# A state-space layer with routed experts: another order of its first tiles, gathers with a lead of four, and one store in five moved

## The chip, the core and the metric

The kernel runs on one core of one Trainium2 chip. Five engines work beside each other: TensorE (PE; PEld is its weight load), VectorE (DVE), ScalarE (ACT), GpSimd (POOL) and SyncE (SP, which here only issues DMAs). The metric is the device time of one execution in microseconds, lower is better. Before the change it is 276.38 us, the median of three runs (275.71 to 276.61).

## What is computed

Four sequences of 512 tokens, 128 wide. `u` is normalized, and two things are computed of it: a state-space layer (its core in the reference below) and a mixture of 16 experts of which each token takes two, with the weights of a softmax over its two best router scores; both are added to `u`.

```python
proj = u @ W_in   # split: z, x, Bg, Cg, dd_dt, dd_A, trap, angles
theta = jnp.cumsum(angles[:, :, None, :] * dt[..., None], axis=1)
K = _rope(Bn[:, :, None, :] + B_bias, theta)
Q = _rope(Cn[:, :, None, :] + C_bias, theta)
S1 = jnp.einsum('bcihn,bcjhn->bcijh', Qc, Kc) * g1c[:, :, None, :, :] * decay
y_inter = jnp.einsum('bcihn,bcih,bchpn->bcihp', Qc, jnp.exp(ell), Hprevs)
y = y + D[None, None, :, None] * x
y = y * jax.nn.silu(z)
return y.reshape(b, L, D_INNER) @ W_out
...
# of each expert e: layernorm((silu(xn @ W1[e]) * (xn @ W3[e])) @ W2[e]) * gamma[e] + beta[e]
```

## The kernel before

The 2048 tokens are 16 tiles of 128 for the state-space part. The expert part sorts the 4096 (token, expert) pairs into 40 blocks of 128 tokens: 32 of one expert, and 8 mixed ones (block 2, 7, 12, ...) of two experts with 64 tokens each. Everything is in one program for each engine, with the order written out by hand; engines wait for each other by semaphores (`wait_ge`), and each engine runs its own list in order.

Three stages follow each other. Up to about 24 us: normalization, router scores, projections. Then the routing on DVE (`one_hots`, `pick_experts`), which sorts the tokens: PE inverts the sort with `invert(k)` over two sets of one-hots, DVE makes of it the lists `gidx` (which token a block gathers) and `sidx` (where its result goes), and `blk_e` (which expert a block has), which starts SP's loads of weights (`load`, four sets in the buffers). Beside it ACT makes the decays of all 16 tiles: tiles 0 to 7 from PE's sums, 8 to 15 from rows that POOL masks (`cut_rows`); PE sums the angles (`sum_turns`), which DVE reduces to `theta` (`cut_turns`).

The third stage weaves tiles and blocks (`weave`, `iteration`): turn t computes tile t of the state-space part and two (even t) or three (odd t) blocks, `b0, b1, b2`. For a block: POOL gathers its tokens from DRAM (`gather`), PE turns it (`turn_block`), ACT copies it (`out_block`), PE multiplies by both up weights (`rise`: the first product goes to ACT's `silu`, the second to DVE's `product`), PE multiplies down (`down`), DVE normalizes (`norm_y`), POOL takes the root (`finish`), DVE scales (`shift_block`) and POOL stores (`store`). For a tile: PE projects (`project_x`, `project_bc`), ACT squares and makes sine and cosine (`squares`, `sines`), POOL `rms_pow` and `rot_sine`, DVE `norm_kq`, `rot_cosine` and `rotate`, PE turns keys and queries (`turn_kq`), then in the next turn `scores`, `inter`, `intra`, where `inter` needs POOL's `weigh_q`. `square_own` (POOL) and `diagonal` (DVE) complete a tile's decay.

Before the change, turn 0 is: block 0 up, tile 0's keys and queries turned, block 1 up, block 0 down. POOL gathers block b + 6 in block b's place (L664), in six buffers (`SLOTS`). The last stage adds the stored results to `acc` and writes the output.

## Time and profile before

| | us |
|---|---|
| median of three runs | 276.38 |
| profiled execution, its own time | 277.72 |
| its span, first to last instruction | 276.0 |
| PE busy | 245.0 (89%) |
| DVE busy | 222.7 (81%) |
| ACT busy | 146.2 (53%) |
| POOL busy | 205.7 (75%) |

The span is the profiled execution's; 1.7 us of its time lie outside it. PE's granted clock is full but for two stretches, 50 to 60 us (0.66 in the mean) and behind 250 us. Shares of the whole span say little of the stretches: the rows below are read by stretch and engine.

### The profile page before, as it was taken

The numbers are of one execution on the slowest core, as the hardware profiler recorded it, in microseconds if no ns is written. First come the engines' busy times: TensorE is split into PE (matmuls) and PEld (weight loads), VectorE is DVE, ScalarE is ACT, GpSimd is POOL, SyncE is SP. The second block draws the span as 40 slices with busy tenths as digits, with TensorE's granted clock in tenths as the row PEclk, the third lists the DMA queues.
The fourth block names the chain that finished last, engine by engine and source line by source line (L and its number), as shares of the span: only waits on it lengthen the run. The fifth ranks groups of instructions, "written<-read, shape, count | busy, mean of one in ns | idle before, by whom it ended". The sixth has DMA issues, their size and how long they took to land.

```text
span 276.0 us, 7214 instructions
## 1 busy us (share of the span) xinstructions
PE 245.0 (89%) x2091; PEld 216.0 (78%) x2094; DVE 222.7 (81%) x596; ACT 146.2 (53%) x492; POOL 205.7 (75%) x279
## 2 busy tenths in 40 slices
PE   2999997499999999999999999999999999998500
PEld 0857964498998898899989979997998899887300
DVE  4768998967979989896989879699889787976446
ACT  1765989546464463737354654636362746452033
POOL 8658997846898979788897978898688786656300
PEclk9999999779999999999999999999999999999855
DMA  6630836976869979878898988788889688870195
GB/s 160 208 114 8 269 119 197 290 200 171 239 224 236 297 219 299 285 226 237 242 285 238 288 255 241 252 239 257 276 238 300 198 269 243 250 200 21 33 296 145
DMA packets 68278, 60.48 MB, mean 219 GB/s; under 512 B 6544, under 2 KB 52240, under 8 KB 68240
## 3 DMA queue, kind: packets, MB, share of 16 engines
q1 hardware_dynamic: 65680, 54.78, 67.1%
q0 software_dynamic: 2560, 5.25, 6.5%
q8 instruction: 17, 0.28, 0.4%
q14 instruction: 21, 0.17, 0.2%
HBM read 55.22 MB, written 4.78 MB: 217 GB/s over the span
## 4 chain that ended last, share of the span: by engine, by line
PE 74%; DMA 6%; ACT 6%; POOL 6%; issue 3%; DVE 2%; SPq 1%; ACTq 0%; POOLq 0%; DVEq 0%
PE bank L897 19%; PE bank L942 10%; PE bank L892 5%; PE bank L838 5%; PE bank L830 4%; ACT decay L1063 3%; PE bank L865 3%; PE bank L813 3%; DMA decay<-l_dram 3%; PE bank L715 3%; PE bank L783 2%; PE bank L820 2%; PE bank L856 2%; PE bank L788 2%; PE bank L938 2%
## 5 line engine op out<-in xcount | busy, mean ns | idle before, releaser
L897 PE MATMUL bank<-blkT,w_up 128*128 128x128 f32 x512 | 65.2, 281 | 1.0 <-ACT blkT L1113 0.8
L897 PEld LDWEIGHTS bank<-blkT,w_up 128*128 128x128 f32 x512 | 61.8, 197 | 2.0 <-issue 0.7
L654 POOL DMA_INDIRECT res_dram<-xrow,sidx x40 | 42.1, 1052 | 20.5 <-DVE xrow L1451 14.0
L597 POOL DMA_INDIRECT blk<-xn_dram,gidx x40 | 42.6, 1066 | 9.3 <-issue 7.0
L942 PE MATMUL bank<-w,xrow 128*128 128x128 f32 x256 | 34.7, 278 | 1.2 <-DVE xrow L1438 1.2
L942 PEld LDWEIGHTS bank<-w,xrow 128*128 128x128 f32 x256 | 31.1, 192 | 2.5 <-issue 2.5
L1119 ACT ACTIVATE xrow<-bank 128x512 f32<-128x512 f32 x40 | 24.4, 609 | 16.3 <-PE bank L897 6.7
L1423 DVE TENSOR_TENSOR xrow<-xrow,bank 128x512 f32<-128x512 f32 x40 | 27.2, 680 | 5.5 <-issue 4.4
L1349 DVE SCALAR_TENSOR_TENSOR kq<-sd,rms,bias_kq 128x512 f32<-128x512 f32 x32 | 22.7, 751 | 6.3 <-issue 5.2
L1113 ACT ACTIVATE blkT<-bank 128x128 f32<-128x128 f32 x40 | 11.5, 287 | 27.9 <-PE bank L883 22.5
L647 POOL TENSOR_TENSOR rstd<-mv,mhalf 128x1 f32<-128x1 f32 x40 | 24.5, 613 | 0.7 <-DVE mv L1435 0.5
L1080 ACT ACTIVATE kqT<-bank 128x512 f32<-128x512 f32 x16 | 9.6, 597 | 29.0 <-issue 18.4
L608 POOL TENSOR_TENSOR rms<-ms,mhalf 128x2 f32<-128x2 f32 x16 | 11.5, 722 | 10.6 <-DVE ms L1338 9.8
L838 PEld LDWEIGHTS bank<-kqT 128*128 128x128 f32 x128 | 15.5, 191 | 3.1 <-issue 3.1
L838 PE MATMUL bank<-kqT 128*128 128x128 f32 x128 | 17.7, 281 | 0.0
L1050 ACT ACTIVATE rot<-bank 128x128 f32<-128x128 f32 x30 | 8.0, 273 | 16.0 <-PE bank L788 12.4
L1451 DVE SCALAR_TENSOR_TENSOR xrow<-xrow,rstd,shift_y 128x128 f32<-128x128 f32 x40 | 13.9, 348 | 2.8 <-POOL rstd L647 2.8
L883 PE MATMUL bank<-ident,blk 128*128 128x128 f32 x40 | 11.8, 294 | 4.8 <-DMA blk<-xn_dram,gidx 4.8
L639 POOL TENSOR_TENSOR qs<-kqT,e_row 128x512 f32<-128x512 f32 x12 | 15.4, 1282 | 0.3
L892 PE MATMUL bank<-w_up,blkT 128*64 128x256 f32 x128 | 15.6, 385 | 0.0
L1103 ACT ACTIVATE x_d<-bank,dskip 128x64 f32<-128x64 f32 x64 | 15.4, 358 | 0.0
L1367 DVE TENSOR_TENSOR rot<-kq,trig 128x256 f32<-128x256 f32 x16 | 14.6, 912 | 0.0
(244 smaller groups left out, 613.5 us busy)
## 6 DMA issues: line engine op xcount, KB each, us to landing
w_up<-in_L_ffn_W_dram SPq DMA_DIRECT2D x96, 256.0 KB
w<-in_L_ffn_W_dram SPq DMA_DIRECT2D x48, 256.0 KB
e_row<-e_dram SPq DMA_DIRECT2D x12, 256.0 KB
decay<-l_dram SPq DMA_DIRECT2D x4, 512.0 KB, 5.7
gam<-in_L_ffn_gamma_dram SPq DMA_DIRECT2D x32, 64.0 KB
shift_y<-in_L_ffn_beta_dram SPq DMA_DIRECT2D x32, 64.0 KB
acc<-in_L_attn_u_dram SPq DMA_DIRECT2D x4, 256.0 KB, 3.7
xn_dram<-xrow SPq DMA_DIRECT2D x4, 256.0 KB, 5.0
```

What stands on the lines that cost most here:

```text
L597: g.indirect_dma_start(out=blk[:, b % SLOTS, :], out_offset=None, in_=xn_dram, in_offset=bass.IndirectOffsetOnAxis(ap=gidx[:, entry(b):ent ...
L639: g.tensor_tensor(qs[:, :], kqT[:, 1, :], e_row[:, j % 2, :], ALU.mult).then_inc(s["qs_ready"], 1)
L647: g.tensor_tensor(rstd[:, :], mv[:, 1:2], mhalf[:, 0:1], ALU.pow).then_inc(f["rstd_ready"], 1)
L654: g.indirect_dma_start(out=res_dram, in_=res[:, b % HALF, :], in_offset=None, out_offset=bass.IndirectOffsetOnAxis(ap=sidx[:, entry(b):ent ...
L838: last = m(bank[2][:, h * P:(h + 1) * P], kqT[:, 0, h * P:(h + 1) * P], kqT[:, 1, h * P:(h + 1) * P], start=True, stop=True)
L892: last = m(bank[out][k * H:(k + 1) * H, lo:hi], blkT[:, b % 2, k * H:(k + 1) * H], w_up[:, u % SETS, n, lo:hi], start=True, stop=True)
L897: last = m(bank[out][:, c * P:(c + 1) * P], w_up[:, u % SETS, n, c * P:(c + 1) * P], blkT[:, b % 2, :], start=True, stop=True)
L942: last = m(bank[7][:, 0:DM], hm[:, b % 2, c * P:(c + 1) * P], w2[:, u % SETS, c, :], start=(c == 0), stop=(c == FC - 1))
L1103: last = a(x_d[:, t % 2, h, :], bank[0][:, h * HD:(h + 1) * HD], ACT.Copy, scale=dskip[:, h:h + 1])
L1119: a(gl, bank[4][:, :], ACT.Silu).then_inc(f["gl_ready"], 1)
L1349: stt(kq[:, q], bc(bn_kq[:, q, :], NH, 0), rms[:, q:q + 1], bias_kq[:, q], ALU.mult, ALU.add)\
L1423: tt(hm[:, b % 2, :], gl, bank[5][:, :], ALU.mult).then_inc(f["hm_ready"], 1)
```

## The change

Constants: `LEAD = 4` (a gather in block b's place is that of block b + 4), `WARM_BLOCKS = 2`.

Routing: `pick_experts` leaves DVE. ACT counts with two Sign activations that have accumulators (`counted`), and POOL does the four small steps behind it; the values are doubled and halved again when `blk_e` is copied, now in the first `one_hots`. PE turns the list in the middle of its decay sums. POOL's 16 products for the angles become 8 of two tiles each. `invert(1)` comes in front of `sum_turns(2)`.

Turn 0: PE does two products that nobody reads, block 0 and block 1 up, block 0 down, then keys, state product and queries (`turn_k`, `turn_q`). ACT copies block 0 in front of its table load; DVE cuts three of the four theta parts first, then normalizes, and does both products in between. POOL gathers block 0 before it cuts the last row, and `square_own(0)` goes behind the gathers. Turn 1 on POOL has a list of its own.

From turn 2 on, POOL: `store(b0 - 3)` stands in even turns behind the rotation, in place of `store(b2 - 2)` at the end of odd turns, in front of `weigh_q`; `finish(b1 - 2)` stands before `square_own`.

Left out of the diff: names of semaphores, small constants, unchanged lines.

```diff
@@ -46,6 +46,8 @@
+    LEAD = 4
@@ -53,12 +55,13 @@
+    WARM_BLOCKS = 2
...
-    CUT = (0, 1, 3, 2)
+    CUT = (0, 1, 2, 3)
@@ -132,7 +135,7 @@
-        bn_kq = sd[:, 0:2, :]
+        bn_kq = sd[:, 2:4, :]
@@ -568,10 +572,19 @@
-            for t in range(NT):
-                last = g.tensor_tensor(turns[:, t, :].rearrange("p (h n) -> p h n", n=NA),
-                                       bc(nar[:, t, 3 * NH:3 * NH + NA], NH, 0), bc(dtp[:, t, :], NA, 1), ALU.mult)
-                if t % TB == TB - 1:
+            pool.wait_ge(counted, 1)
+            g.tensor_scalar(behind[0:NU], full_n[0:NU], NE - 0.5, -2.0 * NE, ALU.is_gt, ALU.mult)
+            link(g.tensor_tensor(full_n[0:NU], full_n[0:NU], mix_n[0:NU], ALU.add))
+            link(g.tensor_tensor(full_n[0:NU], full_n[0:NU], behind[0:NU], ALU.add))
+            g.tensor_scalar(full_n[0:NU], full_n[0:NU], 2.0 * NE, 2.0 * (NE - 1), ALU.add, ALU.min)\
+                .then_inc(expert_ready, 1)
+            for t in range(0, NT, 2):
+                last = g.tensor_tensor(turns[:, t:t + 2, :].rearrange("p t (h n) -> p t h n", n=NA),
+                                       bc(nar[:, t:t + 2, 3 * NH:3 * NH + NA], NH, 1), bc(dtp[:, t:t + 2, :], NA, 2),
+                                       ALU.mult)
+                if t % TB == TB - 2:
                     last.then_inc(turns_ready, 1)
@@ -597,11 +610,13 @@
-            square_own(0)
-            for t in range(SUMMED, NT):
+            for t in range(SUMMED, NT - 1):
                 cut_rows(t)
...
+            gather(0)
+            cut_rows(NT - 1)
             def rms_pow(t):
@@ -617,16 +632,6 @@
-            gather(0)
-            gather(1)
-            rms_pow(0)
-            gather(2)
-            gather(3)
-            rot_sine(0)
-            for b in range(4, SLOTS):
-                gather(b)
-            pool.wait_ge(sidx_ready, 1)
             def weigh_q(t):
@@ -655,27 +660,57 @@
+            def begin():
+                gather(1)
+                rms_pow(0)
+                gather(2)
+                gather(3)
+                square_own(0)
+                rot_sine(0)
+                gather(4)
+                finish(0)
+                square_own(1)
+                pool.wait_ge(sidx_ready, 1)
+            def second_tile():
+                rms_pow(1)
+                gather(5)
+                rot_sine(1)
+                gather(6)
+                finish(1)
+                store(0)
+                square_own(2)
+                gather(7)
+                finish(2)
+                gather(8)
+                weigh_q(1)
+                store(1)
             def iteration(t, first, second, blocks):
...
-                if first and t > 0:
+                if t < 2:
+                    (begin, second_tile)[t]()
+                    return
+                if first:
                     rms_pow(t)
-                if b0 is not None:
-                    finish(b0 - 2)
-                    gather(b0 + SLOTS)
-                if first and t > 0:
+                finish(b0 - 2)
+                gather(b0 + LEAD)
+                if first:
                     rot_sine(t)
-                if b0 is not None:
-                    store(b0 - 2)
+                if t % 2 == 0:
+                    store(b0 - 3)
+                store(b0 - 2)
+                finish(b1 - 2)
...
-                if b1 is not None:
-                    finish(b1 - 2)
-                    gather(b1 + SLOTS)
-                    store(b1 - 2)
+                gather(b1 + LEAD)
+                store(b1 - 2)
...
-                    gather(b2 + SLOTS)
-                    store(b2 - 2)
+                    gather(b2 + LEAD)
@@ -789,29 +824,34 @@
+                if t == SUMMED // 2:
+                    pe.wait_ge(expert_ready, 1)
+                    pe.wait_ge(omb_ready, 1)
+                    nc.tensor.transpose(bank[3][0:1, 0:NU], full_n[0:NU], ident[0:NU, 0:NU]).then_inc(expert_psum, 1)
...
-            pe.wait_ge(expert_ready, 1)
-            pe.wait_ge(omb_ready, 1)
-            nc.tensor.transpose(bank[3][0:1, 0:NU], full_n[0:NU], ident[0:NU, 0:NU]).then_inc(expert_psum, 1)
             sum_turns(1)
+            invert(1)
             sum_turns(2)
-            invert(1)
...
-            def turn_kq(t):
+            def turn_k(t):
...
-                    pe.wait_ge(theta_ready, CUT.index(3) + 1)
...
+            def turn_q(t):
+                if t == 0:
+                    pe.wait_ge(theta_ready, NBATCH)
@@ -929,7 +969,7 @@
-                    pe.wait_ge(theta_ready, NBATCH)
+                    pe.wait_ge(theta_ready, CUT.index(2) + 1)
@@ -943,31 +983,43 @@
+            def begin():
+                pe.wait_ge(sidx_ready, 1)
+                for _ in range(WARM_BLOCKS):
+                    m(bank[6][:, :], ident[:, :], xnT[:, 0:512], start=True, stop=True)
+                turn_block(0)
+                pe.wait_ge(theta_ready, 2)
+                rise(0)
+                turn_block(1)
+                rise(1)
+                turn_block(2)
+                down(0)
+                turn_block(3)
+                turn_k(0)
+                state_product(0)
+                turn_q(0)
             def iteration(t, first, second, blocks):
...
-                begins, ends_ = t == 0, t == NT
-                if begins:
-                    pe.wait_ge(sidx_ready, 1)
-                    turn_block(b0)
-                    pe.wait_ge(theta_ready, 2)
-                    rise(b0)
-                    turn_block(b0 + 1)
-                    turn_kq(t)
-                    turn_block(b0 + 2)
-                elif first:
+                ends_ = t == NT
+                if t == 0:
+                    begin()
+                    return
+                if first:
                     project_x(t)
...
-                if first and not begins:
+                if first:
                     project_bc(t)
...
-                if b0 is not None and not begins:
+                if b0 is not None:
                     rise(b0)
...
-                if b0 is not None and not ends_ and not begins:
+                if b0 is not None and not ends_:
                     down(b0 - 1)
@@ -979,8 +1031,9 @@
-                if first and not begins:
-                    turn_kq(t)
+                if first:
+                    turn_k(t)
+                    turn_q(t)
@@ -1039,6 +1092,11 @@
+            act.wait_ge(ends_ready, 1)
+            a(cmp_f[0:NU], ends[0:NU], ACT.Sign, scale=-1.0, bias=at_full[0:NU, 0:1], accum_out=full_n[0:NU, 0:1])
+            a(cmp_m[0:NU], ends_l[0:NU], ACT.Sign, scale=-1.0, bias=from_mix[0:NU, 0:1], accum_out=mix_n[0:NU, 0:1])\
+                .then_inc(counted, 1)
@@ -1052,7 +1110,7 @@
-                if t == SUMMED + 4:
+                if t == SUMMED + 2:
                     squares(0)
@@ -1064,10 +1122,15 @@
-            def sines(t):
+            def absolutes(t):
...
+            def sines(t):
+                if t > 0:
+                    absolutes(t)
@@ -1098,6 +1161,9 @@
+            def move_x(t):
@@ -1124,29 +1190,43 @@
+            def begin():
+                absolutes(0)
+                out_block(0)
+                nc.scalar.preload_act_table_set("silu_and_others")
+                act.wait_ge(rest_in, 16 * RESTS)
+                sines(0)
+                silu(0)
+                out_block(1)
+                silu(1)
+                out_block(2)
+                weigh(0)
+                move_x(0)
+                gates(0)
+                out_kq(0)
             def iteration(t, first, second, blocks):
...
-                begins = t == 0
-                if begins:
-                    nc.scalar.preload_act_table_set("silu_and_others")
-                    act.wait_ge(rest_in, 16 * RESTS)
-                if first:
+                if t == 0:
+                    begin()
+                    return
+                if t == 1:
+                    squares(t)
                     sines(t)
-                if begins:
+                elif first:
+                    sines(t)
+                    squares(t)
+                if first and t > 1:
                     weigh(t)
-                    gates(t)
-                    out_block(b0)
-                    silu(b0)
-                    out_block(b1)
-                    out_kq(t)
-                elif first:
-                    squares(t)
-                    weigh(t)
-                if b0 is not None and not begins:
+                if b0 is not None:
                     out_block(b0 + 1)
...
-                if first and not begins:
+                if t == 1:
+                    weigh(t)
+                if first:
                     gates(t)
+                    move_x(t)
@@ -1155,7 +1235,7 @@
-                if first and not begins:
+                if first:
                     out_kq(t)
@@ -1211,7 +1291,8 @@
-            tt(at_full, at_full, behind, ALU.min)
+            link(tt(at_full, at_full, behind, ALU.min))
+            ts(at_full, at_full, 0.5, None, ALU.add)
@@ -1254,6 +1335,7 @@
+            ts(from_mix, top[:, 0:1], -1.0, at_mix[:, 0:1], ALU.mult, ALU.add).then_inc(ends_ready, 1)
@@ -1276,33 +1358,25 @@
+            def mean_square(t):
+                dve.wait_ge(s["sq_done"], 2 * (t + 1))
+                again(dve, s["rms_ready"], t)
+                ts(ms[:, :], ms[:, :], 1.0 / DS, EPS, ALU.mult, ALU.add).then_inc(s["ms_ready"], 1)
             def one_hots(k):
...
-                if k == TOPK - 1:
+                if k == 0:
                     dve.wait_ge(expert_psum, 1)
-                    v.tensor_copy(blk_e[:, :], bank[3][0:1, 0:NU]).then_inc(blk_e_ready, 1)
+                    ts(blk_e[:, :], bank[3][0:1, 0:NU], 0.5, None, ALU.mult).then_inc(blk_e_ready, 1)
...
-            def pick_experts():
-                v.tensor_scalar(cmp_f[0:NU], ends[0:NU], at_full[0:NU], None, ALU.is_le)
-                link(ts(limit[0:NU], ends_l[0:NU], top[0:NU, 0:1], None, ALU.add))
-                v.tensor_scalar(cmp_m[0:NU], limit[0:NU], at_mix[0:NU], None, ALU.is_le)
-                link(v.tensor_reduce(full_n[0:NU], cmp_f[0:NU], X, ALU.add))
-                v.tensor_reduce(mix_n[0:NU], cmp_m[0:NU], X, ALU.add)
-                link(ts(behind[0:NU], full_n[0:NU], NE - 0.5, -float(NE), ALU.is_gt, ALU.mult))
-                link(tt(mix_n[0:NU], mix_n[0:NU], behind[0:NU], ALU.add))
-                link(tt(full_n[0:NU], full_n[0:NU], mix_n[0:NU], ALU.add))
-                ts(full_n[0:NU], full_n[0:NU], float(NE - 1), None, ALU.min).then_inc(expert_ready, 1)
             one_hots(0)
-            pick_experts()
             one_hots(1)
+            mean_square(0)
@@ -1317,11 +1391,10 @@
             def cut_turns(b):
-                sums, done = bank[THETA[b]], CUT.index(b)
+                sums = bank[THETA[b]]
...
-                ts(cut, sums[:, :], MAGIC, -MAGIC, ALU.add, ALU.add).then_inc(turns_cut, 1)
-                dve.wait_ge(turns_cut, done + 1)
+                link(ts(cut, sums[:, :], MAGIC, -MAGIC, ALU.add, ALU.add))
@@ -1331,11 +1404,6 @@
-            def mean_square(t):
-                dve.wait_ge(s["sq_done"], 2 * (t + 1))
-                again(dve, s["rms_ready"], t)
-                ts(ms[:, :], ms[:, :], 1.0 / DS, EPS, ALU.mult, ALU.add).then_inc(s["ms_ready"], 1)
             def norm_kq(t):
@@ -1451,33 +1519,41 @@
+            def begin():
+                cut_turns(0)
+                cut_turns(1)
+                cut_turns(2)
+                dve.wait_ge(rest_in, 16 * RESTS)
+                dve.wait_ge(theta_psum, 1)
+                weigh_bc(0)
+                norm_kq(0)
+                cut_turns(3)
+                rot_cosine(0)
+                product(0)
+                rotate(0)
+                product(1)
+                norm_y(0)
+                diagonal(0)
+                diagonal(1)
             def iteration(t, first, second, blocks):
...
-                begins = t == 0
-                if begins:
-                    mean_square(t)
-                    cut_turns(0)
-                    dve.wait_ge(rest_in, 16 * RESTS)
-                    dve.wait_ge(theta_psum, NBATCH)
-                    weigh_bc(t)
-                    cut_turns(1)
-                    norm_kq(t)
-                    rot_cosine(t)
-                    cut_turns(3)
-                    rotate(t)
-                    cut_turns(2)
-                if b0 is not None:
+                if t == 0:
+                    begin()
+                    return
+                if b0 is not None and t > 1:
                     norm_y(b0 - 2)
...
-                if first and not begins:
+                if first:
                     mean_square(t)
...
-                if first and not begins:
+                if first:
                     norm_kq(t)
@@ -1489,11 +1565,9 @@
-                if begins:
-                    diagonal(0)
-                elif first:
+                if first:
                     rot_cosine(t)
-                if first and not begins:
+                if first:
                     rotate(t)
...
```

## Rows read from the trace of the kernel before

**Rows 1.** Windows: us and count busy of each engine, granted clock, DMA share, GB/s.
```profile
120.00:140.00 20.00, 20.00 (x186) 18.57 (x188) 16.64 (x47) 10.06 (x37) 16.98 (x19) 1.00 0.84 241
...
47.00:52.00 5.00, 0.23 (x1) 0.18 (x1) 4.36 (x8) 4.54 (x15) 4.18 (x5) 0.97 1.00 299
52.00:57.00 5.00, 4.59 (x21) 4.40 (x21) 4.93 (x8) 1.15 (x3) 4.21 (x6) 0.50 1.05 300
57.00:64.00 7.00, 7.00 (x55) 6.33 (x55) 3.54 (x11) 3.48 (x13) 1.76 (x3) 0.89 0.64 169
```

**Rows 2.** PE's timeline, 44 to 64 us; in brackets idle time and releaser.
```profile
45.50 1.46 PE L767 MATMUL bank<-pre 128*128 128x384 f32 x6
...
51.77 0.44 PE L883 MATMUL bank<-ident,blk 128*128 128x128 f32 x1 [4.81 <-DMA blk<-xn_dram,gidx]
...
63.06 1.95 PE L892 MATMUL bank<-w_up,blkT 128*64 128x256 f32 x16
```

**Rows 3.** POOL's timeline, 26 to 48 us.
```profile
26.29 7.71 POOL L572 TENSOR_TENSOR pre<-pre 128x128 f32<-128x128 f32 x16
33.95 2.69 POOL L589 TENSOR_SCALAR_AFFINE_SELECT own_sq<-own 128x512 f32<-128x512 f32 x1
...
46.29 1.24 POOL L597 DMA_INDIRECT blk<-xn_dram,gidx  x1 [1.71 <-DVE gidx L1312]
```

**Rows 4.** DVE's timeline, 36 to 54 us.
```profile
36.06 0.60 DVE L1293 TENSOR_SCALAR pre<-pre 48x16 f32<-48x16 f32 x1
...
39.12 1.15 DVE L1283 TENSOR_TENSOR blk<-pre 128x640 f16<-128x640 f16 x1
...
41.37 2.71 DVE L1288 TENSOR_TENSOR rot<-pre 128x2048 f16<-128x2048 f16 x1
...
46.07 0.68 DVE L1323 TENSOR_SCALAR kq<-bank 128x512 f32<-128x512 f32 x1
...
49.65 1.48 DVE L1349 SCALAR_TENSOR_TENSOR kq<-sd,rms,bias_kq 128x512 f32<-128x512 f32 x2 [0.51 <-POOL rms L608]
51.22 0.42 DVE L1366 TENSOR_TENSOR rot<-kq,trig 128x256 f32<-128x256 f32 x1
51.56 2.19 DVE L1367 TENSOR_TENSOR rot<-kq,trig 128x256 f32<-128x256 f32 x1
```

**Rows 5.** ACT's timeline, 27 to 49 us.
```profile
27.53 8.83 ACT L1063 ACTIVATE decay<-bank,lnw 128x128 f32<-128x128 f32 x32 [1.40 <-remote]
37.28 4.79 ACT L1063 ACTIVATE decay<-decay,lnw 128x128 f32<-128x128 f32 x16 [0.92 <-POOL decay L583]
...
47.26 1.28 ACT L1131 ACT_TABLE_LOAD   x1
```

**Rows 6.** The page's costliest groups: busy us, mean ns, idle before them.
```profile
L654 POOL DMA_INDIRECT res_dram<-xrow,sidx x40 | 42.1, 1052 | 20.5 <-DVE xrow L1451 14.0
...
L1423 DVE TENSOR_TENSOR xrow<-xrow,bank 128x512 f32<-128x512 f32 x40 | 27.2, 680 | 5.5 <-issue 4.4
...
L1113 ACT ACTIVATE blkT<-bank 128x128 f32<-128x128 f32 x40 | 11.5, 287 | 27.9 <-PE bank L883 22.5
```

**Rows 7.** Chain that ended last, in order of time: start, us, what.
```profile
15.67 6.92 PE bank L715 x16
...
215.42 1.88 PE bank L892 x16
...
240.60 1.88 PE bank L892 x16
...
253.29 1.28 POOL qs L639
...
258.08 2.30 DMA res_dram<-xrow,sidx
```

**Rows 8.** Waits from 60 to 248 us: total us, times, longest.
```profile
PEld bank L813 <- DVE kq L1373: 1.4, 3, 0.5
```

**Rows 9.** PE's timeline in the steady state.
```profile
138.68 1.95 PE L892 MATMUL bank<-w_up,blkT 128*64 128x256 f32 x16
```

20 lines of the change are left out of this document (10 added, 10 removed).

## The prediction

> **What bounds the kernel now.** I read the stretches first. From about 57 us on TensorE has no gap: in 120:140 it is busy 20.00 of 20 us at full clock, while DVE has 16.64 and POOL 16.98 [rows 1]. There only fewer or earlier matmuls help, and this change has the same matmuls. The stretch in front is different: in 47:52 TensorE is busy 0.23 us, and in 52:57 it works at a granted clock of 0.50, the lower of its two levels, 1.2 GHz [rows 1]. The PE timeline says why: the last theta sum starts at 45.50 and takes 1.46, so PE is done at 46.96, and then it idles 4.81 us until block 0 has landed, turned at 51.77 [rows 2]. The steady state can be dated by the mixed block 2, whose first matmul is at 63.06 [rows 2]; five blocks later the next one comes, and so on. So I ask two things: how much earlier does 63.06 come, and does the steady state or the tail change.
>
> Who makes block 0 late? Its gather starts at 46.29 and takes 1.24, behind 1.71 us in which POOL waited for gidx from DVE [rows 3]. DVE has no gap between 36 and 44 us; within that chain the experts' choice starts at 36.06 and the second set of one-hots at 39.12 [rows 4]. ACT is the other chain: the exponentials of sixteen tiles, four each, then a table load at 47.26 of 1.28 us [rows 5].
>
> **The change, step by step.** The sum is made in the profiled execution: span 276.0, its own time 277.72, so 1.72 lie around the span. The median shown is 276.38, 1.34 under the profiled time; I carry the difference in us over to the median.
>
> 1. *Experts' choice off DVE.* Removed from the routing chain: 39.12 - 36.06 = 3.06 us [rows 4]. Added to it: one 1-column operation behind the scans, and in the first one-hots the copy of blk_e, 0.1 each by the gaps there; I take 0.2. The second lane one-hot (2.71 us from 41.37 [rows 4]) thus ends at 41.2, not 44.1. PE is free for the second inversion then: it had one theta sum (about 2.25 us) between the two inversions where before it had two. So gidx comes 2.8 earlier, and gather 0 starts at 46.29 - 2.8 = 43.5.
>
> 2. *The choice on ACT and POOL.* ACT gets two Sign with accumulators. Before the first exponential it idles 1.40 us [rows 5]; at 0.29 us for a small ACTIVATE [rows 6] and as much again for each accumulator they are at most 1.2, so they are hidden. Bound: 0 to 0.3. POOL gets four operations of one column, 0.3 to 0.6 each, some 1.6 us, while its sixteen products of 7.71 us [rows 3] become eight of twice the width; by what half-size products cost (0.48 each) eight take between 3.9 and 7.7, I take 5.7, so POOL reaches the rows at about 34.2 as before. There own_sq of tile 0 stood (2.69 us from 33.95, most of it while DVE ran its fp16 one-hot [rows 3]); it goes behind the gathers. The first cut row still has to sit out the same one-hot, but is done near 36.5, and the exponentials of the last eight tiles start up to 0.8 earlier than 37.28 [rows 5]. Row 15 is cut behind gather 0, near 45.5, and holds the last tile 0.3 us. ACT is done at 46.7 instead of 47.26. Seven rows fit before 43.5, so POOL doesn't hold the gather.
>
> 3. *Landing of gather 0.* Before, 51.7 - 47.53 = 4.2 us from the end of its issue, with the weights streaming (DMA share 1.00 in 47:52 [rows 1]). Now the weights begin when blk_e is there, some 7 us earlier, so they stream at that time too. The nearest landing without traffic is the last store's, 2.30 [rows 7]. I take 4.1, as the DMA load is alike: landed at 44.7 + 4.1 = 48.8; ends 47.0 and 50. The Trainium skill (DMA: Bandwidth & Descriptors, "SWDGE vs HWDGE vs iDMA") says that the hardware's and the software's queues feed different internal queues of a DMA engine, served in turn; by that a deeper backlog of weights would not hold the gather, and its landing would lie toward the low end.
>
> 4. *Two warming matmuls.* A full 128x512 fp32 product costs 6.92/8 = 0.87 [rows 7]. PE's theta sums end at about 46.3 and sidx is there at 43.3, so the two run 46.3 to 48.0, beside the wait for the gather: cost zero. If the gather lands at 47.0 they cost 1.0. What they bring: the idle time in front of block 0 shrinks from 4.81 to under 1 us, so I expect the clock to stay at 2.4 GHz. Worth: in 52:57 PE was busy 4.59 us at 0.50, which is 2.3 us too long, and in 57:64 at 0.89 another 0.7 [rows 1]. The work from the first turn to block 2 took 63.06 - 51.77 = 11.3, so 8.3 at full clock.
>
> 5. *Two blocks before the keys.* This saves no matmul, it sets which wait is late. Turn 0 at 48.8, ACT's copy, first up product 49.3 to 51.2. ACT now loads its table after that copy, 49.3 to 50.6 [rows 5], and needs 0.6 for the two sines: the cosines are there at 51.2. DVE, from sidx at 43.3: three cuts of 1.35 each (0.68 and as much for the subtraction), the weighing 0.3, norm_kq 1.48, the fourth cut: 50.5; so it waits for ACT. Then the cosine products beside POOL's sine products: 0.42 and 2.19 in the same company before [rows 4], so 51.2 to 53.7, and product(0) of 0.68 [rows 6] until 54.4. PE's second half of block 1 needs that: it idles about 0.9 before block 1 and 1.2 within it. From 54.4: half a block 0.9, down(0) 1.0, turns 0.4, keys 0.44, state 0.85, queries 0.44, the projections 0.9: block 2 at 59.1, ACT's copy of the queries being in time by 0.1. Gain 63.06 - 59.1 = 4.0. Ends: 5.0 when the gather is early and the cosines don't collide, 3.0 when it lands at 50.
>
> 6. *Lead of four.* A gather of block b + 4 is issued some 10 us before its turn and lands in about 4: hidden. The closest is the second tile's gather(5), landed about 1 us before its turn. If that cover is gone it costs once, up to 1 us. The wait of a gather for the turn of an old block goes: worth nothing on the path.
>
> 7. *The third block's store behind the next tile's rotation.* In odd tiles weigh_q comes 1.05 us earlier, in even tiles POOL has one store more, 1.05 [rows 6]; finish(b1-2) moves ahead of square_own there, so for DVE's next shift it comes within 0.3 of before. The next odd tile's rms comes about 0.3 later. PE waits for DVE's rotation three times in all, 1.4 us in sum, mostly hidden [rows 8], so there is little slack but some. Gain: between the mixed blocks at 138.68 [rows 9] and 215.42 [rows 7] lie three periods, each 240.60 - 215.42 = 25.18 where nothing is lost, i.e. 75.5, but 76.7 passed: 1.2 lost, in a chain that goes through store and weigh_q on POOL. I take half back, 0.6; ends 0 and 1.2.
>
> 8. *Tail.* The end hangs on POOL: weigh_q(15) from 253.29, then finish and store of 38 and 39, the last landing from 258.08 on [rows 7]. With store(37) behind finish(38) rather than in front of weigh_q, finish(38) is done 0.5 to 1.1 earlier, and the last store about 0.5 (its predecessor's store is still in the queue). Ends 0 and 0.6.
>
> Sum: 4.0 + 0.6 + 0.5 = 5.1. Span 276.0 - 5.1 = 270.9, profiled time 272.6, median 276.38 - 5.1 = 271.3.
>
> **Rivals.**
> A. *The serial start takes half back.* ACT's copy of block 0 now stands in front of table load and sines, so a late gather delays the rotation too, and with it product(0), both blocks and the keys. For it: DVE's 2.19 us collision [rows 4] and the longer list before product(0). Against: DVE alone would be late (50.5) anyway. A landing at 50 and another us of bubbles leave 2.0 there: 276.38 - 3.1 = 273.3.
> B. *Sign isn't in the active table set.* Then ACT loads two tables in front of the exponentials, 2 x 1.28 [rows 5], of which the idle 1.40 hides little since the Signs use it: 2.2 later on ACT, and PE's sums with it. Time 271.3 + 2.2 = 273.5. The Trainium skill (ScalarE: Activation LUTs, "Table sets: the hidden batching unit") says cheap functions are in every set as filler, without naming Sign among them; by that rule nothing is loaded, and that is why this rival stays small.
> C. *Even tiles' POOL.* If 0.6 of the added store's 1.05 us reached PE in each of the eight even turns from tile 2 on, it would cost 4.8: 276.1, no change. For it: rotations that come just in time [rows 8]. Against: POOL has 3 of 20 us free [rows 1], and every fourth tile has no weigh_q.
> D. *The clock falls all the same, slower.* Its place is the first two blocks. It decides once PE idles before turn 0 about as long as it did, 4.8 us, i.e. if the block lands after 52, or the bubbles in block 1 keep the clock low to block 2. Then the 8.3 us of work take 16.6: block 2 at 65.4 from 48.8, 2.3 later than 63.06, less 1.1 from the rest: 277.6. Against: the warming products, and an idle time of under 1 us.
> E. *Better than forecast.* Landing at 47.5, no collision, all of the stall back: 269.6.
>
> **How the numbers follow.** Forecast 0.60, A 0.18, B 0.04, C 0.08, D 0.06, E 0.04. What a measurement of this kernel can tell from no change is about 0.3%, 0.8 us. Faster by more: forecast, A, B, E = 0.86; within it: C = 0.08; slower: D = 0.06. The likeliest case gives 271.3. Its terms' ends (3.0 to 5.0, 0 to 1.2, 0 to 0.6) span 269.6 to 273.4; A and B lie at its upper edge and somewhat over, so the range is 269.2 to 274.4, and leaves out C and D and a little of A.
>
> **What would show it.** Right: gather 0 at about 43.5; no granted clock below 1 between 47 and 60; block 0's turn near 48.8; the table load between block 0's copy and its silu; product(0) ending near 54.4; block 2 at 59.1; 25.2 from mixed block to mixed block throughout; the last store 0.5 closer to the last mixed block. Wrong: two table loads more at 26 us; a turn of block 0 after 50; periods over 25.3; PE idle in front of the keys' turn in odd tiles, waiting for DVE's rotation.

## The result, and the profile after

| | before | changed |
|---|---|---|
| median, us (runs) | 276.06 (4) | 271.58 (4) |
| lowest to highest | 275.71 to 276.61 | 270.72 to 273.14 |
| profiled execution, its span | 277.72, 276.0 | 270.72, 269.0 |
| PE busy | 245.0 (89%) | 242.5 (90%) |

The changed kernel takes 0.9846 of the time before, 95% interval 0.9801 to 0.9892: 4.5 us less, where 5.1 were forecast, and inside the range. The profiled execution of the changed kernel was its fastest, and that of before was 1.7 over the median of this table, so the two spans differ by 7.0. A second set of runs of the changed kernel (below) gave 271.45 and 0.9825.

Windows of the changed kernel, in the columns of [rows 1]:

```profile
47.00:52.00 5.00, 4.49 (x25) 2.79 (x23) 4.83 (x9) 3.78 (x10) 4.46 (x6) 1.00 0.69 205
52.00:57.00 5.00, 4.40 (x38) 4.21 (x38) 4.12 (x11) 2.87 (x13) 3.21 (x4) 1.00 0.53 154
57.00:64.00 7.00, 6.96 (x57) 5.89 (x57) 5.21 (x13) 6.25 (x25) 4.54 (x7) 1.00 0.55 148
120.00:140.00 20.00, 20.00 (x177) 18.46 (x175) 16.35 (x45) 9.81 (x38) 16.40 (x20) 1.00 0.89 270
```

Where PE had 0.23 us of work in 47:52, it has 4.49; where its clock was 0.50, it is 1.00. PE's timeline, beside [rows 2] (kernel lines of after: L923 a block's turn, L937 up, L932 up of a mixed block, L982 down, L990 the warming products, L848 and L860 the turns of keys and queries):

```profile
45.85 1.46 PE L802 MATMUL bank<-pre 128*128 128x384 f32 x6
47.15 1.88 PE L990 MATMUL bank<-xnT,ident 128*128 128x512 f32 x4
49.13 0.33 PE L923 MATMUL bank<-ident,blk 128*128 128x128 f32 x1
...
52.39 1.16 PE L937 MATMUL bank<-blkT,w_up 128*128 128x128 f32 x8 [0.39 <-ACT blkT L1179]
53.76 1.16 PE L937 MATMUL bank<-blkT,w_up 128*128 128x128 f32 x8 [0.21 <-DVE xrow L1491]
...
55.87 0.60 PE L848 MATMUL bank<-ident,kq 128*128 128x128 f32 x4
...
58.67 1.70 PE L932 MATMUL bank<-w_up,blkT 128*64 128x256 f32 x13
```

No idle time stands before block 0's turn (4.81 in [rows 2]), and block 2 starts at 58.67, not 63.06: 4.39 gained. In front of it lie DVE, POOL and ACT; their timelines, in this order, beside [rows 3 to 5]:

```profile
32.38 1.12 DVE L1370 TENSOR_TENSOR blk<-pre 128x640 f16<-128x640 f16 x1
...
39.56 2.71 DVE L1375 TENSOR_TENSOR rot<-pre 128x2048 f16<-128x2048 f16 x1
42.20 0.60 DVE L1364 TENSOR_SCALAR ms<-ms 128x2 f32<-128x2 f32 x1
...
43.41 0.57 DVE L1386 TENSOR_SCALAR gidx<-pre 128x40 int32<-128x40 f32 x1
```
```profile
28.30 5.68 POOL L584 TENSOR_TENSOR pre<-pre 128x256 f32<-128x256 f32 x8
33.94 10.01 POOL L596 TENSOR_SCALAR_AFFINE_SELECT decay<-decay 128x512 f32<-128x512 f32 x7
44.87 1.25 POOL L610 DMA_INDIRECT blk<-xn_dram,gidx  x1 [0.92 <-DVE gidx L1386]
```
```profile
46.83 1.28 ACT L1121 ACTIVATE decay<-decay,lnw 128x128 f32<-128x128 f32 x4 [0.41 <-POOL decay L596]
...
49.50 0.28 ACT L1179 ACTIVATE blkT<-bank 128x128 f32<-128x128 f32 x1 [1.19 <-PE bank L923]
49.79 1.28 ACT L1197 ACT_TABLE_LOAD   x1
51.08 0.31 ACT L1136 ACTIVATE trig<-theta 128x128 f32<-128x128 f32 x1
```

Gather 0 starts 1.42 earlier than before, not 2.8. The second gain is in the steady state. The eight mixed blocks start at these times (PE's timelines; in brackets the distance):

```
before    63.06  88.31(25.25) 113.50(25.19) 138.68(25.18) 163.78(25.10) 188.96(25.18) 215.35(26.39) 240.53(25.18)  sum 177.47
changed   58.67  83.85(25.18) 108.53(24.68) 133.71(25.18) 158.37(24.66) 183.55(25.18) 208.21(24.66) 233.38(25.17)  sum 174.71
```

Every other period can be 24.66: it holds an even tile (4, 8, 12) in which the recurrence starts anew and one group of products is left out. The kernel before paid 25.10 to 26.39 there. The changed one pays nothing anywhere: 2.76 less. What the kernel before pays isn't the same each time: in a profile in which only its first products differ (the warming products, below) its periods sum to 176.23, so that the gain against it is 1.5. The end takes back 0.55: from the last mixed block to the issue of the last store 17.55 before (258.08 [rows 7] less 240.53), 18.10 after (251.48 less 233.38). POOL's timeline at the end, and a line of DVE's:

```profile
244.39 1.26 POOL L644 TENSOR_TENSOR qs<-kqT,e_row 128x512 f32<-128x512 f32 x1
247.09 0.54 POOL L652 TENSOR_TENSOR rstd<-mv,mhalf 128x1 f32<-128x1 f32 x1 [1.44 <-DVE mv L1503]
...
251.48 1.03 POOL L659 DMA_INDIRECT res_dram<-xrow,sidx  x1 [0.68 <-DVE xrow L1519]
```
```profile
244.45 1.35 DVE L1519 SCALAR_TENSOR_TENSOR xrow<-xrow,rstd,shift_y 128x128 f32<-128x128 f32 x1 [0.47 <-POOL rstd L652]
```

The last tile's weighing of q (L644) no longer stands behind the store of block 37. It starts 11.0 after the last mixed block, not 12.8, and meets DVE's shift of block 37, which takes 1.35 and not 0.35; PE waits 1.97 for what follows (1.17 before). Block 38's root still comes a little earlier than before (13.71 after the last mixed block, not 13.98), but POOL now has two stores instead of one between it and block 39's root. So the spans are accounted for: 4.39 + 2.76 - 0.55, and 0.4 from the last loads, is 7.0.

### The profile page after: what moved, and what is told of

The parts are those of the page before. It is cut to its first block, busy times and chain, and to the rows that moved or that the text cites. A ratio compares the mean times of both kernels' runs of the same rounds, so it can differ in the third digit from the quotient of the medians.

```text
span 269.0 us, 7214 instructions
## 1 busy us (share of the span) xinstructions
PE 242.5 (90%) x2095; PEld 213.6 (79%) x2098; DVE 216.7 (81%) x589; ACT 146.8 (55%) x496; POOL 203.4 (76%) x276
## 4 chain that ended last, share of the span: by engine, by line
PE 74%; DVE 10%; POOL 5%; issue 3%; DMA 3%; ACT 3%; SPq 1%; POOLq 0%; ACTq 0%; DVEq 0%
PE bank L937 20%; PE bank L982 11%; PE bank L932 6%; PE bank L878 6%; PE bank L870 4%; PE bank L905 3%; PE bank L818 3%; PE bank L978 3%; PE bank L860 2%; PE bank L848 2%; PE bank L823 2%; PE bank L896 2%; PE bank L914 2%; DMA decay<-res_dram 2%; PE bank L923 2%
## 5 line engine op out<-in xcount | busy, mean ns | idle before, releaser
L937 PE MATMUL bank<-blkT,w_up 128*128 128x128 f32 x512 | 63.1, 276 | 1.0 <-issue 0.4
L937 PEld LDWEIGHTS bank<-blkT,w_up 128*128 128x128 f32 x512 | 60.0, 192 | 1.6 <-ACT blkT L1179 0.6
L659 POOL DMA_INDIRECT res_dram<-xrow,sidx x40 | 41.3, 1032 | 14.6 <-DVE xrow L1519 7.4
L982 PE MATMUL bank<-w,xrow 128*128 128x128 f32 x256 | 34.8, 279 | 2.0 <-DVE xrow L1506 2.0
L982 PEld LDWEIGHTS bank<-w,xrow 128*128 128x128 f32 x256 | 31.1, 192 | 3.3 <-DVE xrow L1491 2.1
L652 POOL TENSOR_TENSOR rstd<-mv,mhalf 128x1 f32<-128x1 f32 x40 | 22.9, 572 | 3.7 <-DVE mv L1503 3.1
L1519 DVE SCALAR_TENSOR_TENSOR xrow<-xrow,rstd,shift_y 128x128 f32<-128x128 f32 x40 | 17.5, 437 | 3.7 <-POOL rstd L652 3.7
L1364 DVE TENSOR_SCALAR ms<-ms 128x2 f32<-128x2 f32 x16 | 5.3, 334 | 13.5 <-ACT rot L1108 13.5
L932 PE MATMUL bank<-w_up,blkT 128*64 128x256 f32 x128 | 15.6, 385 | 0.0
L644 POOL TENSOR_TENSOR qs<-kqT,e_row 128x512 f32<-128x512 f32 x12 | 15.4, 1281 | 0.3
L1506 DVE SCALAR_TENSOR_TENSOR xrow<-bank,mv,gam 128x128 f32<-128x128 f32 x40 | 14.0, 351 | 0.3 <-issue 0.3
```

Source lines behind the costliest of these rows:

```text
L644: g.tensor_tensor(qs[:, :], kqT[:, 1, :], e_row[:, j % 2, :], ALU.mult).then_inc(s["qs_ready"], 1)
L652: g.tensor_tensor(rstd[:, :], mv[:, 1:2], mhalf[:, 0:1], ALU.pow).then_inc(f["rstd_ready"], 1)
L659: g.indirect_dma_start(out=res_dram, in_=res[:, b % HALF, :], in_offset=None, out_offset=bass.IndirectOffsetOnAxis(ap=sidx[:, entry(b):ent ...
L932: last = m(bank[out][k * H:(k + 1) * H, lo:hi], blkT[:, b % 2, k * H:(k + 1) * H], w_up[:, u % SETS, n, lo:hi], start=True, stop=True)
L937: last = m(bank[out][:, c * P:(c + 1) * P], w_up[:, u % SETS, n, c * P:(c + 1) * P], blkT[:, b % 2, :], start=True, stop=True)
L982: last = m(bank[7][:, 0:DM], hm[:, b % 2, c * P:(c + 1) * P], w2[:, u % SETS, c, :], start=(c == 0), stop=(c == FC - 1))
```

## Experiments

The first four ran in one set (before: 276.38), four in a second (276.19), four in a third (275.84). Each is read against before of its own set; the intervals are of 95%. The theory: the start hangs on the chain one-hots, gather, turn; the steady state on whether POOL's and DVE's operations meet.

**The changed kernel once more**, unchanged.

> The changed kernel itself, beside the variants of this set, so that they are compared on one chip. Expected: 271.6 (271.0 to 272.4), block 2 at 58.7, seven periods between mixed blocks of 25.18 and 24.66 in turn, 174.7 from the first mixed block to the last. If its periods vary from run to run as those of the variants did (25.5, 25.3), the lossless sequence of its first profile was partly luck; then the sum is nearer 175.6.

Measured: 271.45 (270.76 to 272.13), 0.9825 (0.9795 to 0.9854). The periods are the same to 0.02 (sum 174.73), so being lossless was no luck. Block 2 started at 60.04: here gather 0, issued at 44.96, landed late.

```profile
50.48 0.33 PE L923 MATMUL bank<-ident,blk 128*128 128x128 f32 x1 [0.97 <-DMA blk<-xn_dram,gidx]
```

From the end of its issue (46.21) that is 4.3 us; in the first profile it was at most 3.0.

**Is the routing chain what counts?** Ten small linked operations on DVE, where the experts' choice had stood:

```
             one_hots(0)
+            for _ in range(5):
+                link(ts(zer, zer, 1.0, None, ALU.mult))
+                link(ts(limit, limit, 1.0, None, ALU.mult))
             one_hots(1)
```

> The changed kernel with ten small linked operations on VectorE (about 0.2 each, 2.0 to 2.5 together) between the one-hots of the first and the second choice, where the choice of the experts stood before the change. Nothing reads what they write. Theory (steps 1 and 3 of the prediction): this chain sets gather 0, and with it the first turn of a block; gather 0 goes from 44.9 to about 47.2, block 0's turn from 49.1 to about 51.3, TensorE idles 2.2 to 3 before it, block 2 starts 2.2 later at 60.9, or 3.5 to 4 later where the clock falls; time 273.7, up to 275. Rival: the theta sums on TensorE and what VectorE does behind the one-hots are late anyway, block 2 is at most 1 later, time 272 to 272.5; then most of the start's gain is the two blocks ahead of the keys.

Measured: 276.09, 1.0001 (0.9975 to 1.0027), above the forecast's 273.7 to 275: the whole gain is gone. The ten took 4.4 us, not 2.0 to 2.5, as six of them ran at 0.55 to 0.60 each beside POOL's row cuts. Gather 0 went to 47.82, 2.95 later, and block 2 to 63.98, 5.3 later. The difference, about 2.4, is PE's clock; the variant's windows, and its PE timeline:

```profile
42.00:47.00 5.00, 1.47 (x17) 1.03 (x18) 4.17 (x9) 3.41 (x12) 0.00 (x0) 0.69 0.76 226
47.00:52.00 5.00, 5.00 (x12) 3.00 (x11) 4.37 (x10) 1.48 (x5) 3.77 (x5) 0.63 0.71 206
```
```profile
45.53 0.71 PE L810 MATMUL bank<-blk,rot 128*128 128x40 f16 x16 [4.07 <-DVE rot L1375]
46.08 2.06 PE L800 MATMUL bank<-pre,sd 128*128 128x512 f32 x2
```

PE idled 4.07 for the second one-hots, and then did the theta sums at the half clock (2.06 for what takes 1.02 to 1.10), so block 0's turn came at 54.49. Of 4.4 us of chain 2.95 reached the gather, and yet the median is 4.5 to 4.6 over the changed kernel's two. The low clock makes the difference, by a way that no theory had named: not block 0 is late, but PE itself.

**The warming products.** Left out of the changed kernel (`WARM_BLOCKS = 0`), and put into the kernel before:

> The changed kernel without the two products in front of block 0. Theory W: they keep the clock up and cost nothing, since the gather lands when they end. Then without them PE idles from 47.3 to about 49, the clock stays at full anyway or falls for a part of the first two blocks, and block 2 comes at 58.7 to 61. Rival D: they delay turn 0, because the gather had landed at about 48: then turn 0 comes 0.5 to 1.3 earlier than 49.1; since the idle time is then only about 1 us the clock holds, and block 2 comes up to 1 us earlier. Medians: by W 271.6 to 273, by D 270.6 to 271.6.

> The kernel before with only the two products in front of block 0's turn. PE's idle time there was 4.81 us; the products take 1.9, so 2.9 remain. Theory W: the clock then stays at full through the first blocks and the start gains what the low clock had cost, 2.5 to 3.0 us: block 2 at 60.3 instead of 63.1, median 273.3. Rival P: in that order of turn 0 the work waits for the other engines (silu, product, rotation), so that a faster PE gains at most 1 us: block 2 at 62, median 275.3. Rival N: an idle time of 2.9 us still lowers the clock: no change, 276.1.

Measured: without them 272.77, 0.9871 (0.9838 to 0.9905); in the kernel before 275.96, 0.9998 (0.9964 to 1.0031). PE's timeline and the windows of the changed kernel without them, then PE's timeline of the kernel before with them:

```profile
50.12 0.30 PE L923 MATMUL bank<-ident,blk 128*128 128x128 f32 x1 [2.33 <-DMA blk<-xn_dram,gidx]
```
```profile
47.00:52.00 5.00, 2.25 (x16) 1.88 (x15) 4.86 (x9) 3.00 (x7) 4.30 (x6) 1.00 0.83 237
52.00:57.00 5.00, 4.41 (x37) 3.98 (x36) 3.64 (x8) 2.86 (x12) 3.48 (x4) 1.00 0.50 154
```
```profile
51.79 0.47 PE L883 MATMUL bank<-ident,blk 128*128 128x128 f32 x1 [3.13 <-DMA blk<-xn_dram,gidx]
52.67 3.75 PE L897 MATMUL bank<-blkT,w_up 128*128 128x128 f32 x16 [0.41 <-issue]
```

With 2.33 us idle the clock held at 2.4 GHz; with 3.13 idle it fell to 1.2, in spite of the products (3.75 where 2.02 is full speed). So in this kernel the earlier gather holds the clock, and the products aren't needed for it in this profile. Leaving them out costs 0.7 to 1.3 us (0.9871 against 0.9846 and 0.9825, with intervals that overlap). In the profile 0.9 of that lies in the periods (sum 175.61), and none of it in the clock of the start: block 2 starts at 59.64, among those of the changed kernel. The trace shows the place: in the three even turns the weighing of q starts 0.15 to 0.17 after the mixed block, where it starts 0.08 to 0.10 before it in both profiles of the changed kernel, and the rotated keys come later by as much, 0.25. Why it starts later there stays open.

**Keys first.** The changed kernel with one block in front of the keys; ACT and DVE follow:

```
                 turn_block(1)
-                rise(1)
+                turn_k(0)
+                turn_q(0)
                 turn_block(2)
+                rise(1)
                 down(0)
                 turn_block(3)
-                turn_k(0)
                 state_product(0)
-                turn_q(0)
```

> The changed kernel with only one block in front of the first keys, as before the change: order rise 0, block 1's turn, keys, q, block 2's turn, rise 1, down 0. ScalarE and VectorE follow (key/query copy before block 2's copy, rotation before the product of block 0). Theory (step 5 of the prediction): the two blocks fill the wait for the rotated keys; without them TensorE waits for the keys 2 us or more near 51 to 54, product of block 0 comes 1.5 us later, and block 2 starts 1 to 2 us later, at 59.9 to 60.7; time 272.8 to 273.4. Rival: the whole start gain comes from the earlier gather and from choosing the experts off VectorE; then block 2 stays within 0.4 of 58.7 and the time within 0.3 of the changed kernel.

Measured: 273.75, 0.9917 (0.9885 to 0.995), 2.3 longer than the changed kernel. Block 0 turned at 49.35, as early as it could, and block 2 began at 60.52, for PE waited on the rotated keys (its timeline):

```profile
54.76 0.66 PE L848 MATMUL bank<-ident,kq 128*128 128x128 f32 x4 [2.59 <-DVE kq L1442]
```

The second block is what fills this wait. The theory holds for block 2 (59.9 to 60.7 expected); the median is 0.35 over its price. Its profiled execution took 272.93, 0.9 more than the changed kernel's in the same set, so the rest of the median's 2.3 isn't seen in a trace. The clock was 1.00 after 2.59 idle.

**The moved store, from both sides.** First the move alone in the kernel before, then the changed kernel without it:

```
+                if t % 2 == 0:
+                    store(b0 - 3)
                 ...
                     gather(b2 + SLOTS)
-                    store(b2 - 2)
```

> The kernel before with only the third block's store moved behind the next turn's rotation. Theory S: the distance between mixed blocks 2 and 37 falls from 177.5 to about 174.8 in the profile; the median falls by 1 to 2.7 us, to 273.4 to 275. Rival L (the lead or the order of finish did it, or two stores in a row in even turns cost as much as they save): 177 and more, median 275.7 to 276.5.

> The changed kernel with only the third block's store back at the end of its own odd turn, in front of weigh_q (turn 1 gets store(2) there too). Theory S: the store's place is what made the steady state shorter: between mixed blocks 2 and 37 the changed kernel needs 174.8 us and the kernel before 177.5, and the losses of before (0.5, 0.4, 1.7) stand in the periods in which an even turn follows that has no weigh_q, where POOL's rms_pow came late. Then this kernel's distance is 176.5 to 178, its median 1.5 to 2.7 above the changed kernel's, about 273.5, and POOL's rms_pow in turns 4, 8 and 12 waits behind the store. Rival L: the lead of four or finish(b1-2) in front of square_own did it; then the distance stays at 174.8 and the median within 0.5 of the changed kernel's.

Measured: in the kernel before 276.58, 1.0005 (0.9971 to 1.0039), periods' sum 176.61; the changed kernel without the move 273.44, 0.9899 (0.9864 to 0.9934), sum 177.41, with periods of up to 26.13. So the move alone brings nothing, and its absence costs 1.5 to 2.0, by the shares of before against those of the changed kernel's two sets. 0.95 of the 2.7 that the periods lose lies in the first one, where the edit also puts the stores of blocks 1 and 2 in front of the second tile's weighing of q. What goes with the move? In the changed kernel the second block's rstd also comes before the next tile's square mask. The changed kernel with that one swap undone, and the kernel before with both:

```
                 store(b0 - 2)
-                finish(b1 - 2)
                 if t + 1 < NT:
                     square_own(t + 1)
+                finish(b1 - 2)
                 gather(b1 + LEAD)
```

> The changed kernel, in which only GpSimd's order in a turn goes back in one place: the square mask of the next tile stands before the second block's rstd again, not behind it. The third block's store stays moved. Theory 'both together': the store's move alone gave nothing in the order of the kernel before (0.9998 to 1.0005 of its time), and without the move the changed kernel lost 2.7 in its periods; so the rstd's earlier place carries part of the lossless periods, and without it they come to 175.5 to 176.6 in place of 174.7, the time to 272.3 to 273.4. Rival 'the store alone': periods stay 25.18 and 24.66 in turn, time within 0.3 of the changed kernel's 271.5; then what the store's move lacked in the kernel before is something else.

> The kernel before with both changes of GpSimd's order in the steady turns and nothing of the start: the third block's store goes to the next turn, and the second block's rstd comes before the square mask. Theory: with both the periods come to 174.7 (25.18 and 24.66 in turn), 1.9 less than with the store's move alone (176.6), block 2 stays near 62 to 63, and the time is 2 to 2.8 under the kernel before: 273.4 to 274.2. Rival: the lead of six blocks (three gathers in front of their use, in GpSimd's turns) or the start's state carries on, the periods stay at 176 to 177 and the time within 0.5 of the kernel before's 276.3.

Measured: swap undone 272.39, 0.9886 (0.9852 to 0.992), sum 176.85, short periods of 24.97 to 25.00 and a last one of 26.35. The kernel before with both: 274.4, 0.9959 (0.9926 to 0.9993), sum 174.70, as lossless as the changed kernel, though its time fell by 1.4 and not by 2 to 2.8. Part of the rest is the tail, which is 18.10 long here too (17.55 before). It needs both, and it gets there with the start and the lead of before. (The 0.9998 in the first of the two expectations is the ratio of the kernel before with warming products.) DVE's and POOL's timelines in the same even turn, first of the changed kernel, then with the swap undone (their mixed blocks start at 83.85 and 84.55):

```profile
89.66 0.43 DVE L1434 TENSOR_TENSOR rot<-kq,trig 128x256 f32<-128x256 f32 x1
90.01 0.41 DVE L1435 TENSOR_TENSOR rot<-kq,trig 128x256 f32<-128x256 f32 x1
90.46 0.74 DVE L1441 TENSOR_TENSOR kq<-rot 128x256 f32<-128x256 f32 x1
91.12 0.86 DVE L1442 TENSOR_TENSOR kq<-rot 128x256 f32<-128x256 f32 x1
...
83.77 1.28 POOL L644 TENSOR_TENSOR qs<-kqT,e_row 128x512 f32<-128x512 f32 x1
```
```profile
90.55 0.87 DVE L1434 TENSOR_TENSOR rot<-kq,trig 128x256 f32<-128x256 f32 x1
91.35 0.86 DVE L1435 TENSOR_TENSOR rot<-kq,trig 128x256 f32<-128x256 f32 x1
92.24 0.43 DVE L1441 TENSOR_TENSOR kq<-rot 128x256 f32<-128x256 f32 x1
92.58 0.42 DVE L1442 TENSOR_TENSOR kq<-rot 128x256 f32<-128x256 f32 x1
...
84.67 1.28 POOL L644 TENSOR_TENSOR qs<-kqT,e_row 128x512 f32<-128x512 f32 x1
...
91.21 0.71 POOL L602 TENSOR_SCALAR_AFFINE_SELECT own_sq<-own 128x512 f32<-128x512 f32 x1
```

The rotated keys are 0.32 later (8.45 after the mixed block, not 8.13), and the period is longer by the same 0.32. Two parts make it up. DVE begins 0.19 later (6.00, not 5.81), and that comes from the end of the turn before: with the swap undone the weighing of q starts 0.12 after the mixed block, not 0.08 before it, DVE's `ms` ends 0.03 to 0.04 after the weighing in both, and POOL's root and DVE's scaling of the keys follow. The other 0.13 is the meeting itself, which moves rather than goes away: in the changed kernel the two halves take 0.43 and 0.41 and the two operations behind them 0.74 and 0.86 beside the mask; with the swap undone it is 0.87 and 0.86, then 0.43 and 0.42. That is how one root behind the mask instead of in front of it costs PE a third of a us.

**A lead of six.** Here the second tile has two gathers more before its q is weighed:

```
-    LEAD = 4
+    LEAD = 6
                 ...
                 gather(8)
+                gather(9)
+                gather(10)
                 weigh_q(1)
```

> The changed kernel with gathers six blocks ahead instead of four; tile 1 issues two gathers more (about 1.05 us of GpSimd each) before its q weighing. Theory 'the lead is only cover' (step 6 of the prediction): same time as the changed kernel within 0.3, periods unchanged, possibly block 2 to 4 some tenths later in the first odd tile, where GpSimd has 2.1 us more to do. Rival 'the lead keeps transfers off the start': six gathers before the first turns of blocks collide with the landing of blocks 1 and 2, TensorE waits for blocks from DMA between 50 and 57 and the time is 0.5 to 1 longer.

Measured: 273.43, 0.9921 (0.9881 to 0.9961), 2.0 longer. Neither theory: block 0 wasn't late (48.95). The first two periods lost 1.54 and 0.66, the later ones nothing. POOL weighs q 14.5 us after block 2's start instead of 11.9, the next tile's rms comes behind it at 78.03, and DVE waits 1.49 before it scales the keys, until that rms is done (78.76; the row names no releaser). PE waits for the product queued behind (timelines of DVE and PE):

```profile
78.85 1.41 DVE L1419 SCALAR_TENSOR_TENSOR kq<-sd,rms,bias_kq 128x512 f32<-128x512 f32 x2 [1.49 <-issue]
```
```profile
81.18 1.16 PE L939 MATMUL bank<-blkT,w_up 128*128 128x128 f32 x8 [1.28 <-DVE xrow L1493]
```

**The tail.** The last odd tile alone in the old order:

```
-                if t % 2 == 0:
+                if t % 2 == 0 and t < NT:
                     store(b0 - 3)
                 ...
+                if t == NT - 1:
+                    store(b2 - 2)
                 if first:
                     weigh_q(t)
```

> The changed kernel, but in the last odd tile alone the third block's store stays in its own turn, before the q weighing, as in the kernel before. Theory: the tail lost 0.6 because in turn 16 GpSimd took up two stores and the q scaling later, so that its q scaling ran against VectorE's shift of block 37 (1.35 us instead of 0.35) and held the product of block 39; with the old order the way from the last mixed block to the last store goes from 18.10 back to about 17.55 and the time falls 0.5 to about 271.1. Rival: the collision is chance, and the last odd tile gets the conflict on the key/query path instead (0.5 to 1.7 us as in the periods of the kernel before); then the tail is as long or longer, and the time is the same or 0.5 more.

Measured: 271.45, 0.983 (0.9797 to 0.9863); the changed kernel beside it had the same 271.45. From the last mixed block (234.09) to the last store (251.66) it is 17.57, as forecast, but from there to the end 18.14, where the run beside it had 17.42. SyncE's issue of the final loads, which starts as soon as the last store is in, lasted 6.32 us instead of 5.62 in the trace. Over all profiles this last stretch varies from 17.0 to 18.1, so half a us in the tail is seen in the trace and not in this median.

**Parting the first collision, with the tail's edit.** With the changed kernel's start the second half of block 1 waits 0.21 or 0.22 in three profiles and 1.23 to 1.33 in four others, the four in which block 0 turned earliest (48.80 to 48.95). Timelines of DVE and POOL in the variant just shown, one of the four:

```profile
51.58 1.91 DVE L1436 TENSOR_TENSOR rot<-kq,trig 128x256 f32<-128x256 f32 x1
```
```profile
51.18 0.65 POOL L602 TENSOR_SCALAR_AFFINE_SELECT own_sq<-own 128x512 f32<-128x512 f32 x1
51.80 0.72 POOL L632 TENSOR_TENSOR rot<-kq,trig 128x256 f32<-128x256 f32 x1
52.49 0.72 POOL L633 TENSOR_TENSOR rot<-kq,trig 128x256 f32<-128x256 f32 x1
```

DVE comes at 51.58, while POOL's mask is still running (to 51.83), and its product of 0.43 lasts until POOL's next two are over as well (53.2) and 0.3 more. In the first profile of the changed kernel DVE began at 51.82, when the mask was ending, and POOL's first product at 51.88: DVE's took 0.43, and POOL's 0.94. So 0.2 us decide it. Putting a gather between them parts the two; the tail's edit comes with it. The edit, beside that one:

```
                 square_own(0)
-                rot_sine(0)
                 gather(4)
+                rot_sine(0)
                 finish(0)
```

> The changed kernel with the fourth gather ahead of GpSimd's half of the first rotation, and the last odd tile in the old order. Theory 'the port goes to whoever comes first': VectorE's first half of the rotation started at 51.58 while GpSimd was busy, and was held 1.91 until GpSimd's two products had ended, in four of the runs; where it started at the same time as GpSimd, or ahead, it took 0.43. With the gather between, GpSimd's products start about 53.1, VectorE's rotation takes 0.43 and 0.41 and ends near 52.5, the product of block 0 ends near 53.1, TensorE's 0.2 to 1.24 before the second half of block 1 is gone, and block 2 starts at 58.4 to 58.7 in every run: time 270.6 to 271.0, 0.5 to 0.8 less than the changed kernel. Rival: the keys become late instead: GpSimd's products end at 54.5 and VectorE's last part of the rotation ends after 55.9, TensorE waits 0.3 to 0.6 for the keys, and the gain is gone (271.4).

Measured: **270.0** (269.52 to 270.47), 0.9789 (0.9762 to 0.9817), 0.6 under the forecast's low end. It was not run beside the changed kernel: its median is 1.5 under that kernel's two, its gain over before of its own set 1.1 to 1.4 more than theirs, and all five runs lie under all ten of theirs, but the intervals of the ratios overlap. DVE's timeline:

```profile
51.99 0.43 DVE L1436 TENSOR_TENSOR rot<-kq,trig 128x256 f32<-128x256 f32 x1 [0.27 <-ACT trig L1140]
52.34 0.42 DVE L1437 TENSOR_TENSOR rot<-kq,trig 128x256 f32<-128x256 f32 x1
52.67 0.68 DVE L1493 TENSOR_TENSOR xrow<-xrow,bank 128x512 f32<-128x512 f32 x1
```

The product of block 0 ends at 53.35 (54.42 in the profile above), and block 2 starts at 58.39 though its gather was 0.3 late. The Trainium skill (SBUF — State Buffer, "Who interferes with whom") says that VectorE and GpSimd share one pair of ports which whoever issues first holds for the whole instruction. The traces agree for these pairs: 1.91 when GpSimd's mask is running as VectorE comes, 0.43 when VectorE is ahead of GpSimd's product. They add one thing: VectorE, there before the two products, had to wait for both behind the mask.

## Why the prediction was right, point by point

*1, choice off DVE*: right in what it removes, too large in what arrives. Of the 3.06 taken off, 1.8 reached the second inversion: the one-hots began 0.54 later (32.38; 31.84 before) and the first set took 0.6 more beside POOL's wider products and row cuts, 0.1 of it the copy of `blk_e`. Then gidx's cast took 0.57 where it took 0.18 before. Gather 0 came at 44.87, not 43.5: the term was 1.42, not 2.8. That a shorter chain on DVE would run beside other POOL work, and so slower, is what the step left out.

*2, the choice on ACT and POOL*: hidden, as said, and no table load, so rival B is out. But row 15 was cut at 46.14 and ACT was done at 48.1, not 46.7; the 1.19 it then waited for block 0 covered that.

*3, landing*: 4.1 assumed; at most 3.0 in the first profile, 4.3 in the second. The bounds (2.3 to 5.3) were right for these two; in the kernel before with both orders it was 5.6. By the rule of the Trainium skill weighed there (DMA: Bandwidth & Descriptors, "SWDGE vs HWDGE vs iDMA") the landing would lie near the low end each time; the 4.3 speaks against relying on it.

*4, warming*: zero cost and no low clock, as said. That the products hold the clock was wrong as a cause: it held without them over 2.33 us. What they bring in the median, 0.7 to 1.3, isn't the 3.0 of the clock.

*5, two blocks before the keys*: block 2 at 58.67 and 60.04 (59.1 forecast), and 59.37 to 59.40 in the three variants with this start. In the first profile the gather came 1.4 later than forecast, but landed 1.1 faster, and the way from block 0's turn to block 2 was 9.54 long instead of 10.3, as the bubbles were 0.39 and 0.21 and not 0.9 and 1.2: errors that cancelled. The 2.19 taken for DVE's collision is one of two outcomes; where it happens the way is 10.6. The step's pieces from 54.4 on also add up to 4.93 and not to 4.7, so that by its own numbers block 2 starts at 59.3 and the gain is 3.7 (the trace has 4.97 from the end of block 0's product at 53.70).

*6, the lead*: counted as nothing. For transfers that is right (no block was late), for POOL it isn't: in the second tile two gathers less are worth 2.0 in the medians, 1.7 if the three runs at a low clock (below) are left out.

*7, the store*: this is the term that was mis-sized: 0.6, and 2.76 came in the profiled pair. I took 25.18 for the lossless period everywhere, while every other one can be 24.66, so of the loss before I saw 1.2 in three periods, where it was 2.2, and 2.8 in all seven. And the step gave the store alone what it does only together with the earlier rstd. In the median the two bring 1.4 by the kernel before with both, the longer tail included.

*8, the tail*: wrong in sign: 0.55 lost, not 0.5 gained. The rstd of block 38 came 0.27 earlier and not 0.5 to 1.1, since DVE's shift met POOL's weighing of q, a place that the step had not looked at. And from there to the last store it is 4.39 instead of 3.57, since POOL has two stores and not one before the rstd of block 39, which the step noted and didn't price.

Of the sum 4.5 to 4.7 arrived in the medians. Block 2 started at 61.64, 63.06, 63.09 and 63.42 in the four profiles with the start of before, and at 59.4 in the mean of the five with exactly the changed one and a full clock: 3.4 from the start, where 4.0 were forecast. The new order brought 1.4 in the kernel before, with the tail's loss in it, so about 1.9 in the periods, where 0.6 were forecast, and -0.5 in the tail, where it was +0.5. The three errors, -0.6, +1.3 and -1.0, nearly cancel. The places of the gain were foreseen; that the sum came out within 0.6 is in part luck. Of rival A, a late landing came once (second set), but without the bubbles that it needed; C is out (even turns with two stores lose nothing), and D did not happen, though the run with the longer chain, its gather 3 us later, shows a low clock again.

## What to carry to other kernels

When a change moves an operation of GpSimd or VectorE, list what runs on the other of the two at its new time: in this kernel one misplaced meeting cost PE 0.3 to 1.1 us. Work out the lossless length of each period from its own products before you call a period lossless. And a delay in front of an idle TensorE can cost more than its own length when the wait lowers the clock for the work behind it: here a gather 2.95 us later came with a block 2 that was 4.6 to 5.3 later.
